# A decoder kernel: ternary feed-forward work moved to ScalarE and GpSimd, and an expert layer's scores, search and shared expert rearranged

## The reference, cut to what matters

```python
def _act_quant(x):
    scale = 127.0 / jnp.clip(jnp.max(jnp.abs(x), axis=-1, keepdims=True), 1e-05)
    return jnp.clip(jnp.round(x * scale), -128.0, 127.0) / scale
def _bitlinear(x, w):                       # w: 512x128, rounded to -1, 0, 1 times one scale
    return jnp.einsum('bsi,oi->bso', _act_quant(x), _weight_quant(w))
# L1_ffn
gate = jax.nn.silu(_bitlinear(x, w_gate)); up = _bitlinear(x, w_up)
return _bitlinear(gate * up, w_down)
# L2_ffn: h is layernorm(x), 8192x128, 16 experts, cap = 1024
scores = jax.nn.sigmoid(h @ gate_w.T)
topk_score, topk_ids = jax.lax.top_k(scores.T, cap)
...                                         # the chosen tokens through the experts, scattered back
shared = silu(h @ sh_gate_w.T) * (h @ sh_up_w.T) @ sh_down_w.T      # sh_*: 256 wide
return out + shared
```

## Time and profile before

| | |
|---|---|
| median of 3 runs | 5404.78 us (5399.6 to 5406.33) |
| the profiled execution | 5424.38 us, span 5422.6 us, mean granted TensorE clock 0.867 |
| PE / PEld / DVE / ACT / POOL busy | 77% / 62% / 57% / 37% / 42% of the span |
| stage L1_ffn, first moments to last residual | 2326.88 to 2598.99 |
| stage L2_ffn, pass / score transfers / search | 3336.14 to 3473.67 / to 3483.94 / to 3573.15 |

### The profile page before, as it was taken

How to read it: one execution, slowest core, us unless ns; L and a number is a source line. 1 busy time by engine, 2 the same in 40 slices (tenths; PEclk the granted TensorE clock), 3 DMA queues, 4 the chain that set the end, 5 groups by cost and what they waited for, 6 DMA issues and landing times. The chain is left out here.

```text
span 5422.6 us, 287237 instructions
## 1 busy us (share of the span) xinstructions
PE 4196.6 (77%) x120935; PEld 3342.5 (62%) x120944; DVE 3092.1 (57%) x11142; ACT 1999.3 (37%) x5449; POOL 2280.5 (42%) x4326
## 2 busy tenths in 40 slices
PE   6999977253999877734899898618885998889987
PEld 5877764132666666612677786414554887778866
DVE  3555558432444677789555555574333656776656
ACT  3554446010434333323444453102222553335622
POOL 3443422275333566600233442006884446664510
PEclk9999988555999876666899998859997999999989
DMA  3000002433000111100000001203442000000001
GB/s 85 5 6 18 17 21 58 76 62 73 2 0 0 25 30 29 28 8 0 2 0 4 19 19 28 54 13 75 74 74 43 0 2 19 17 12 1 0 2 31
DMA packets 379912, 139.86 MB, mean 26 GB/s; under 512 B 216118, under 2 KB 372870, under 8 KB 379430
## 3 DMA queue, kind: packets, MB, share of 16 engines
q1 hardware_dynamic: 344822, 107.59, 8.5%
q0 software_dynamic: 34816, 28.34, 3.8%
HBM read 91.45 MB, written 43.85 MB: 25 GB/s over the span
## 5 line engine op out<-in xcount | busy, mean ns | idle before, releaser
L980 DVE TENSOR_REDUCE rowmax<-ps 128x16 f32<-128x1024 f32 x512 | 627.0, 1225 | 758.0 <-PE ps L639 758.0
L658 PE MATMUL ps<-qT,kblock 32*64 32x64 f32 x36864 | 972.5, 233 | 44.2 <-issue 38.1
L658 PEld LDWEIGHTS ps<-qT,kblock 32*64 32x64 f32 x36864 | 803.3, 138 | 94.3 <-issue 45.8
L639 PE MATMUL ps<-kblock,qT 32*64 32x128 f32 x16384 | 811.0, 298 | 9.8 <-issue 9.5
L521 POOL TENSOR_TENSOR vareps<-meanvar,eps 128x1 f32<-128x1 f32 x576 | 133.1, 231 | 1595.1 <-DVE negmean L954 1595.1
L682 PE MATMUL ps<-v,probT 64*64 64x64 f32 x36864 | 794.0, 233 | 2.4 <-ACT probT L858 1.1
L858 ACT ACTIVATE probT<-ps 128x1024 f32<-128x1024 f32 x512 | 523.7, 1023 | 700.8 <-PE ps L669 700.6
L682 PEld LDWEIGHTS ps<-v,probT 64*64 64x64 f32 x36864 | 710.8, 146 | 102.3 <-issue 99.4
L558 POOL TENSOR_TENSOR kblock<-kT,key_scale 128x512 f32<-128x512 f32 x576 | 599.9, 1042 | 39.0 <-ACT kT L840 27.1
L639 PEld LDWEIGHTS ps<-kblock,qT 32*64 32x64 f32 x16384 | 485.1, 139 | 145.7 <-issue 119.9
L844 ACT ACTIVATE xn<-x_res,nmr,rstd 128x128 f32 (+1 forms) x512 | 252.9, 494 | 501.7 <-POOL nmr L528 501.2
(11 more groups left out here) (353 smaller groups left out, 9297.0 us busy)
## 6 DMA issues: line engine op xcount, KB each, us to landing
ctxT<-in_ctxT SPq DMA_DIRECT2D x256, 64.0 KB, 1.9
held<-in_g_w SPq DMA_DIRECT2D x16, 836.0 KB, 4.8
ctxT<-in_ctxT SPq DMA_DIRECT2D x256, 32.0 KB, 1.9
table<-prob SPq DMA_DIRECT2D x32, 256.0 KB, 2.4
x_dram<-x_res SPq DMA_DIRECT2D x32, 256.0 KB, 2.4
x_res<-x_dram SPq DMA_DIRECT2D x16, 512.0 KB, 7.2
x_res<-in_x SPq DMA_DIRECT2D x8, 512.0 KB, 7.1
x_res<-in_e_w SPq DMA_DIRECT2D x64, 64.0 KB, 1.8
```

The costliest lines, as they stand in the source:

```text
L639: mm = nc.tensor.matmul(k.s1[S * b:S * b + S, g % 2, at:at + 2 * S].rearrange("p (h s) -> p h s", h=2), k.qT[rows, buf, S * b:S * b + S], ...
L658: mm = nc.tensor.matmul(out, k.kblock[rows, buf, h, S * b:S * b + S], k.qT[rows, buf, S * b:S * b + S], start=not part.softmax or (first a ...
L980: nc.vector.tensor_reduce(spread, heads, AX.X, ALU.max).then_inc(soft.did["max_raw"], 1)
```

## The change

In `bitlinear_pass` the depth becomes 5. GpSimd takes over variance + eps (VectorE keeps bn_stats and bn_aggr, now `quad_moments`) and makes the negative mean times the reciprocal deviation (`quad_scale`); ACT normalises (Identity with scale and bias) and also makes x·(127/max)+MAGIC, GpSimd takes MAGIC off, clips and casts, for x (one of 128x512 a quad) and for the hidden quad (four of 128x512). `b_h` and `b_hq` get two copies each, in `k.held`. DVE's step is now: residual it-4, moments it, maximum and scale it-1, gate product, maximum, scale and product plus MAGIC it-2. PE: gate and up it-2, transposes and down it-3, transposes of x it-1. ACT: silu it-2, x plus MAGIC it-1, hidden copies it-3, normalisation it, copy of the transposed x it-1. GpSimd: hidden rounding it-3, `quad_scale` it, x rounding it-1; `pool_pause` is a tiny operation ahead of a group.

`shared_pass` becomes `score_pass`: normalisation on ACT as in the stage above, transposes, a copy into `k.held` that is kept for all 16 quads, one matmul for transposed scores, a sigmoid, a transfer of them to DRAM for each quad, and four small identity matmuls that turn them back for the token table. On each engine the blocks of older quads stand ahead: DVE copies the scores of it-2 before the moments of it; PE does the scores' transposes of it-2, the score matmul of it-1, then the transposes of it. There is no shared expert and no transfer of x in it.

`choose_tokens` has one transfer at its head. The search takes sixteen steps of two bits with three candidates each (the first all zeros), so 48 counts of 128x1024, written as bf16 instead of f32. Each step also holds the shared expert of a quad: gate and up of it and down of it-1 on PE, silu on ACT, the product with up (it-1) and the residual (it-2) on DVE, and the transfer of x (it-2) on SP. The end of it is unchanged.

```diff
+def quad_scale(k, pool, m, it, par):
+    nc, g = k.nc, m * TILES + 4 * it
+    pool.wait_ge(k.f_mv, g + 4)
+    mean = k.q_meanvar[:, par, :, 0:1].rearrange("p q o -> p (q o)")
+    variance = k.q_meanvar[:, par, :, 1:2].rearrange("p q o -> p (q o)")
+    nc.gpsimd.tensor_tensor(k.q_vareps[:, par, :], variance, k.eps[:, 0:1].broadcast_to([P, 4]),
+                            ALU.add).then_inc(k.f_var, 4)
+    nc.gpsimd.tensor_tensor(k.q_negmean[:, par, :], mean, k.minus_one[:, 0:1].broadcast_to([P, 4]),
+                            ALU.mult).then_inc(k.f_neg, 1)
+    pool.wait_ge(k.f_var, g + 4)
+    nc.gpsimd.tensor_tensor(k.q_rstd[:, par, :], k.q_vareps[:, par, :], k.half_power[:, 0:1].broadcast_to([P, 4]),
+                            ALU.pow).then_inc(k.f_rstd, 4)
+    pool.wait_ge(k.f_rstd, g + 4)
+    pool.wait_ge(k.f_neg, it + 1)
+    nc.gpsimd.tensor_tensor(k.q_nmr[:, par, :], k.q_negmean[:, par, :], k.q_rstd[:, par, :],
+                            ALU.mult).then_inc(k.f_nmr, 1)
...
+                if active(it, 3, ends):
+                    t, b = it - 3, 1 - par
+                    pool.wait_ge(k.b_hchain, HL * t + HL)
+                    if positive(4 * (t - 1)):
+                        pool.wait_ge(k.b_hT_psum, 4 * (t - 1))
+                    pool_pause(k, pool, k.b_pause_h, 5, t)
+                    for q in range(4):
+                        nc.gpsimd.tensor_scalar(k.b_hq[:, b, q, :], k.b_h[:, b, q, :], MAGIC, QMAX, ALU.subtract,
+                                                ALU.min).then_inc(k.b_hq_done, 1)
                 if active(it, 0, ends):
-                    quad_pool(k, pool, m, it, par)
-            tile_pipeline(pool, step, 3, count=QUADS)
+                    quad_scale(k, pool, m, it, par)
+                if active(it, 1, ends):
+                    t, b = it - 1, 1 - par
+                    pool.wait_ge(k.b_xr_done, 4 * t + 4)
+                    if positive(t - 1):
+                        pool.wait_ge(k.b_xT_psum, t - 1)
+                    pool_pause(k, pool, k.b_pause_x, 6, t)
+                    nc.gpsimd.tensor_scalar(k.b_xq[:, b, :], k.b_xn[:, b, :], MAGIC, QMAX, ALU.subtract,
+                                            ALU.min).then_inc(k.b_xq_done, 1)
+            tile_pipeline(pool, step, 5, count=QUADS)
...
+                if active(it, 4, ends):
+                    t, b = it - 4, par
+                    dve.wait_ge(k.b_down, 4 * t + 4)
+                    for q in range(4):
+                        xt = k.x[:, bass.ds((4 * t + q) * P, P)]
+                        nc.vector.scalar_tensor_tensor(xt, ps[:, 6, q * P:(q + 1) * P], k.b_hscale[:, b, q:q + 1], xt,
+                                                       ALU.mult, ALU.add).then_inc(k.b_res, 1)
...
                 if active(it, 1, ends):
                     t, b = it - 1, 1 - par
+                    count = Count(t, QL)
+                    amax = k.b_xmax[:, b, :]
+                    dve.wait_ge(k.f_xn, m * TILES + 4 * t + 4)
+                    nc.vector.tensor_reduce(amax, k.b_xn[:, b, :].rearrange("p (q c) -> p q c", q=4), AX.X, ALU.max,
+                                            apply_absolute_value=True).then_inc(k.b_qchain, 1)
+                    dve.wait_ge(k.b_qchain, count.next())
+                    if positive(4 * t):
+                        dve.wait_ge(k.b_xr_done, 4 * t)
+                    scale_up(dve, k.b_qchain, count, amax, k.b_xinv[:, :])
+                    assert count.passed == QL
...
-                    dve.wait_ge(k.b_hchain, after)
-                    for q in range(4):
-                        if positive(4 * t + q - 3):
-                            dve.wait_ge(k.b_hT_psum, 4 * t + q - 3)
-                        nc.vector.tensor_scalar(k.b_hq[:, q, :], k.b_h[:, q, :], MAGIC, QMAX, ALU.subtract,
-                                                ALU.min).then_inc(k.b_hq_done, 1)
-                if active(it, 0, ends):
...
-                    quad_norm(k, dve, m, k.x, it, par, xn)
...
-                    for q in range(4):
-                        nc.vector.tensor_scalar(xn[:, q * P:(q + 1) * P], xn[:, q * P:(q + 1) * P], k.b_xinv[:, q:q + 1],
-                                                MAGIC, ALU.mult, ALU.add).then_inc(k.b_qchain, 1)
-                        after = count.next()
-                    assert count.passed == QL
...
-                    nc.vector.tensor_scalar(k.b_xq[:, par, :], xn, MAGIC, QMAX, ALU.subtract,
-                                            ALU.min).then_inc(k.b_xq_done, 4)
...
+                    act.wait_ge(k.b_qchain, QL * (t + 1))
...
+                        xn = k.b_xn[:, b, q * P:(q + 1) * P]
+                        nc.scalar.activation(xn, xn, ACT.Identity, scale=k.b_xinv[:, q:q + 1],
...
+                    act.wait_ge(k.f_nmr, it + 1)
+                    if positive(it - 1):
+                        act.wait_ge(k.b_xq_done, it - 1)
+                    nc.scalar.activation(k.pause_act[:, 0:1], k.eps[:, 0:1], ACT.Copy)
+                    for q in range(4):
+                        nc.scalar.activation(k.b_xn[:, par, q * P:(q + 1) * P], k.x[:, bass.ds((4 * it + q) * P, P)],
+                                             ACT.Identity, scale=k.q_rstd[:, par, q:q + 1],
+                                             bias=k.q_nmr[:, par, q:q + 1]).then_inc(k.f_xn, 1)
...
+                if active(it, 2, ends):
+                    t, b = it - 2, par
+                    dve.wait_ge(k.logit_ready, t + 1)
+                    if positive(8 * (t - b)):
+                        dve.wait_ge(k.w_out_ready[b], 8 * (t - b))
+                    nc.vector.tensor_copy(k.r_score[:, b, 0:4 * E], ps[:, b, 0:4 * E]).then_inc(k.score_ready, 1)
                 if active(it, 0, ends):
-                    quad_stats(k, dve, m, k.x, it, par)
...
+                if active(it, 2, ends):
+                    t, b = it - 2, par
+                    pe.wait_ge(k.r_scoreT, t + 1)
+                    if positive(t - 1):
+                        pe.wait_ge(k.score_ready, t - 1)
                     for q in range(4):
+                        mm = nc.tensor.matmul(ps[:, b, E * q:E * (q + 1)], scoreT[:, b, q * P:(q + 1) * P], k.ident[0:E, 0:E],
                                               start=True, stop=True)
                     mm.then_inc(k.logit_ready, 1)
+                if active(it, 1, ends):
+                    t, b = it - 1, 1 - par
+                    pe.wait_ge(k.f_xT, front + 4 * t + 4)
+                    if positive(t - 1):
+                        pe.wait_ge(k.r_scoreT, t - 1)
+                    nc.tensor.matmul(ps[0:E, 2 + b, :], k.router[r.name][:, :], k.held[:, bass.ds(t * QW, QW)], start=True,
+                                     stop=True).then_inc(k.r_logitT, 1)
                 if active(it, 0, ends):
                     pe.wait_ge(k.f_xn, m * TILES + 4 * it + 4)
+                    if positive(it - 1):
+                        pe.wait_ge(k.f_xT, front + 4 * it - 4)
                     for q in range(4):
+                        mm = nc.tensor.transpose(ps[:, 6 + par, q * P:(q + 1) * P], k.q_xn[:, par, q * P:(q + 1) * P], k.ident)
                     mm.then_inc(k.f_xT_psum, 4)
             tile_pipeline(pe, step, 3, count=QUADS)
...
+                    nc.scalar.activation(scoreT[:, b, :], ps[0:E, 2 + b, :], ACT.Sigmoid).then_inc(k.r_scoreT, 1)
...
+                    nc.scalar.activation(k.held[:, bass.ds(it * QW, QW)], ps[:, 6 + par, :], ACT.Copy).then_inc(k.f_xT, 4)
...
-            sp.dma_start(k.score_dram, k.held[0:r.E, :]).then_inc(k.c_io, 16)
+            sp.dma_start(score, k.score_dram.rearrange("e (c n) -> (e c) n", c=8)).then_inc(k.c_io, 16)
...
-            with dve.Fori(0, 30) as bit:
-                count = Count(bit, 4)
-                nc.vector.tensor_tensor(cand.bitcast(I32), thr.bitcast(I32), k.bits[:, bass.ds(bit, 1)],
-                                        ALU.bitwise_or).then_inc(k.c_chain, 1)
-                dve.wait_ge(k.c_chain, count.next())
-                nc.vector.tensor_scalar(work, score, cand, None, ALU.is_ge, ALU.add, accum_out=k.c_count[:, 0:1]).then_inc(k.c_chain, 1)
-                dve.wait_ge(k.c_chain, count.next())
-                dve.wait_ge(k.c_psum, bit + 1)
-                nc.vector.tensor_scalar(cand, ps[:, 0, 0:1], cap, cand, ALU.is_ge, ALU.mult).then_inc(k.c_chain, 1)
-                dve.wait_ge(k.c_chain, count.next())
-                nc.vector.tensor_tensor(thr, thr, cand, ALU.max).then_inc(k.c_chain, 1)
-                dve.wait_ge(k.c_chain, count.next())
+            dve.wait_ge(k.c_io, 16)
+            thr, cand, reached, best = k.c_thr[:, 0, :], k.c_cand[:, :], k.c_reached[:, :], k.c_best[:, :]
+            def step(it, par, ends):
+                if active(it, 0, ends):
+                    count = Count(it, CC)
+                    nc.vector.tensor_tensor(cand.bitcast(I32), thr.bitcast(I32).broadcast_to([P, 3]),
```

(63 more changed lines are left out.)

427 lines of the change are left out of this document (143 added, 284 removed).

## The result

The changed kernel takes 5376.5 us (median of 7 runs, 5369.1 to 5387.6), the kernel before 5402.3 in 7 runs beside it: a ratio of 0.995, with a 95% interval of 0.9937 to 0.9962. So it is some 26 us faster, with 5382 forecast. The two profiled executions are 47.9 us apart (spans 5422.6 and 5374.7), which is more than the medians are. Part of the surplus has nothing to do with the change: the code ahead of the ternary pass is the same in both, and the pass starts at 2326.9 in the one and at 2315.3 in the other. In the twelve traces of the experiments it starts between 2310.9 and 2325.1. So I read stages by their own length, not by the time at which they stand. These lengths repeat well: the changed kernel's ternary pass takes 219.8 to 221.1 us in the six traces that hold it unchanged.

The account below looks back on a forecast made before the run. VectorE was taken to bound the ternary pass, TensorE the expert pass. Ternary -45.9, score pass -5.5, transfer -6.4, search +35.3 sum to -22.5: 5401.9 on the profiled execution, 5382 on the runs' scale; range 5350 to 5414.

Parts of the forecast that it names:

- the price of a rounding: Ternary pass: one 128x512 rounding on GpSimd takes 1.15 us, lower bound 0.86, upper bound 1.6.
- It cannot be the bound by work alone: Ternary pass: GpSimd's work per quad, about 8 us or 10.4 at most, stays below VectorE's 12.1.
- The period that I had, 13.5: Ternary pass: time per quad in us, VectorE's 12.1 of work plus 1.4 of waits.
- 1.4 of waits behind GpSimd's operations: Ternary pass, per quad: VectorE operations held 1.2 us with what follows, and 0.2 more behind the x rounding.
- The ends: Ternary pass: filling and draining beyond the sixteen periods, put at 10.2 us where 8.9 was.
- The port rule: VectorE and GpSimd share an SBUF port pair as an exclusive lock; whoever comes second blocks fully.
- The loop of the prediction: Score pass: identity matmuls, score copy, moments, GpSimd's operations, normalisation and transposes bound each quad, 7.0 us at full clock.
- my 8.5 for the lower clock level: Score pass: time per quad in us with TensorE at about half clock, 1.5 more than at full clock.
- the 7.9: Score pass: period in us taken between 7.0 and 8.5, nearer the low clock, giving a pass of 132.0.
- the 5.5 us of gain: Score pass: 132.0 us where it was 137.5; 19 less at full clock, nothing at half.
- 7.5: Search: us per step, taken between 7.15 and TensorE's 7.9 at clock 0.72; sixteen steps and draining make 124.5.
- Rival (c): Search: bound by TensorE at half clock, 11.4 us a step, 62 us more, 5444 in all; chance 9%.

Follow-up runs that it names:

- gates alone: Changed kernel with TensorE's fourth gate matmul ahead of the third up matmul, GpSimd keeping all five roundings; ternary stage 220.8 us, period 12.8 on the mean.
- x rounding gone: Changed kernel with the x rounding moved from GpSimd to ScalarE behind the hidden copies, TensorE's order kept; ternary stage 207.5 us, period 11.85.
- the closed timeline: Changed kernel with x rounding on ScalarE behind the hidden copies and the fourth gate matmul before the third up; 0.9905 of before, ternary stage 199.2 us.

## Why the prediction came out right, point by point

**Ternary pass.** 220.6 for 226.2, but that is luck: three errors met, a rounding priced too low, waits and work of VectorE too high, and ends too short. The term that failed is the price of a rounding: 1.92 to 2.04 where I took 1.15 and set 1.6 as the upper bound. The row by columns, 0.55 times four, gave 2.2, and that was the near one; I had weighted the L558 row because it has as many columns, but a different operation stands in it. The step that fell with it is "It cannot be the bound by work alone": five of them and the small operations are 12.56, and that sets the period (gates alone: nothing; x rounding gone: 11.85). The period that I had, 13.5, I had built from VectorE's 12.1 and 1.4 of waits behind GpSimd's operations. VectorE's work is 11.3, as the closed timeline above shows. Of the 0.8 between, 0.56 are waits for silu in the earlier trace rows's quad that I had carried along as work: the gate product takes 3.42 there, from 2501.49 to 2504.91, and 2.86 in the closed timeline.

```profile
2501.49 2.46 DVE L1171 SCALAR_TENSOR_TENSOR prob<-ps,b_scale,prob 128x512 f32<-128x512 f32 x3
...
2504.16 0.75 DVE L1171 SCALAR_TENSOR_TENSOR prob<-ps,b_scale,prob 128x512 f32<-128x512 f32 x1 [0.21 <-ACT prob L1304]
```

The lengthening is there at the places where I put it, but its sum is 0.5 in the small operations and up to 0.35 in the four products, not 1.4. The ends went the other way: sixteen periods of 12.7 leave 17 of the 220.6, where I had put 10.2. The last residual waits 8.87 for its down matmuls, which stand behind four bare roundings of 7.91, not 4.6.

**The port rule.** The Trainium skill ("SBUF — State Buffer", section "Who interferes with whom") has the engine that comes second block fully, with VectorE in its two-port mode. The traces don't show a full block for these operations: beside roundings of 1.92 the four-element operations take at most 0.56, and where they start elsewhere in the same roundings 0.17 at the median. Whether they meet the page's condition no run shows. The long maxima of the earlier trace rows are real but don't carry over. What decides who waits how long was not isolated.

**Score pass.** The loop of the prediction is the one the trace shows, and the experiments opened it link by link. The size: 8.45 a quad, which is my 8.5 for the lower clock level; the granted clock was 0.50 throughout. The term that failed is the 7.9, a middle between two clock levels of which only one appeared, and so the 5.5 us of gain were -0.7. My range around it was also summed wrong: 8.5 in the same sum gives 140.4, which is 3 us more than before and not nothing, and 7.0 gives 18 less, not 19. What I didn't ask is whether the loop had to be there: I counted it as the price of fewer matmuls.

**Transfer.** 3.4 us where 3.9 were forecast.

**Search.** 109.5 for 124.5, the largest miss in us. A step is 6.34 and 6.74 in turn, 6.54 on the mean, where I had 7.5:

```profile
3457.84 0.16 DVE L2052 TENSOR_TENSOR c_cand<-c_thr,bits 128x3 int32<-128x3 int32 x1
3458.03 1.28 DVE L2056 TENSOR_SCALAR_CACHE_REDUCE kblock<-prob,c_cand 128x1024 bf16<-128x1024 f32 x1
...
3459.24 1.28 DVE L2056 TENSOR_SCALAR_CACHE_REDUCE kblock<-prob,c_cand 128x1024 bf16<-128x1024 f32 x1
...
3464.58 0.16 DVE L2052 TENSOR_TENSOR c_cand<-c_thr,bits 128x3 int32<-128x3 int32 x1 [0.55 <-DVE c_thr L2078]
```

Of the 0.96, 0.35 are the clock: TensorE ran at 0.99 in a stretch in which it is busy 80 of 90 us, so its 5.7 us of matmuls stayed off the path and the step is VectorE's. 0.24 are the two added counts, which start 1.20 apart, not 1.32; that is the spacing of the two counts at the end of the search of before (3573.15 and 3574.47), where the second waits for the first. Another 0.18 are the product and the residual, which take 1.13 and 0.60 of the chain (they start at 3461.76 and 3462.89, the next instruction at 3463.49) instead of 1.22 and 0.69. The 0.2 left I can't assign. Rival (c) wanted the lower level here; it appeared only in the first 7 us (0.50 from 3413 to 3420). bf16 as the output of a count changed nothing: 1.276 us against 1.279.

**The sum.** 37.4 by stages for 22.5, and 26 by the medians. That the forecast's 5382 lies as close as it does to 5376.5 is thus partly luck: the stages gave 15 us more than forecast, and the difference between the medians has 11 us less than the stages.

## What to carry to other kernels

When work moves to an idle engine, price it by the nearest row of the same operation scaled by its columns, and add up that engine's whole step; if the sum comes near the bound's, as 12.56 here against the 12.1 I had for VectorE, expect it to become the bound. In a software pipeline where each engine works in order, follow one quad's chain through every engine's order and look for a link that goes from an older quad back to a newer one: here exchanging two pairs of blocks, with no work removed, gave 58 us, over twice what the whole change gave. And an edit that removes a wait shows nothing while another engine binds: the gate order was worth 0 alone and 8 us behind the other edit.

## What the runs showed of the hardware that was not expected

A GpSimd `tensor_scalar` of 128x512 from f32 to bf16 takes 1.92 us with two operations and 1.49 with one, against 0.43 for the same work on VectorE and 0.72 for a rounding by activation, without the clip, on ScalarE. TensorE stayed at its lower clock level in a pass in which it was busy 56 of 100 us. With the loop open it was busy without a gap from 3300 to 3330 and granted 0.50 all the time, then had the full level for some 7 us, waited 0.8 to 1.2 us a quad in them, and fell back; over 3300 to 3350 that makes 0.58. In the changed kernel's search, busy 80 of 90 us, it had 0.99.
